# A Mamba decoder layer on one core: the first of sixteen products of each scan step on ScalarE

## The chip, the cores and the metric

The kernel runs on one NeuronCore of a Trainium2 chip. The metric is the device time of one execution in microseconds (us); the kernel before takes 3092.49 us (median of three runs). TensorE (PE) multiplies matrices, VectorE (DVE), ScalarE (ACT) and GpSimd (POOL) do elementwise work, and SyncE (SP) issues the transfers. Each engine runs its own program in order; they meet at semaphores.

## What is computed

The reference is a decoder layer with three parts: a selective state space layer (Mamba), a cross attention, and a small gated LoRA, each followed by a layer norm over a residual sum. The input has 16 sequences of 128 tokens with 1024 features. The change touches the state space part alone. There, with D_IN = 2048 channels and N = 16 states a channel:

```python
dt = jax.nn.softplus(ts @ W_dt.T + b_dt)
A = -jnp.exp(A_log.astype(jnp.float32))

def step(state, inp):
    dt_t, B_t, C_t, u_t = inp
    dA = jnp.exp(dt_t[..., None] * A)
    state = state * dA + (dt_t * u_t)[..., None] * B_t[:, None, :]
    y = jnp.einsum('bdn,bn->bd', state, C_t)
    return (state, y)
```

So the output of a channel at a token is a sum over 16 state indices: y = sum over n of C[n] times state[n]. The product at n = 0 starts this sum, the fifteen others add to it.

## The kernel before

The 16 sequences go in 4 groups of 4 (`GB = 4`), the 2048 channels in 16 tiles of 128. A scan step `s` of the program (there are `NS = 16`) is one group with four channel tiles (`QD = 4`), and within it an unrolled loop runs over the state index `n` from 0 to 15. For each index:

- POOL (`pool_step`, L1085) writes dt·u·B for the four tiles into one of four buffers `hb`.
- ACT (`act_step`, L937) writes four exponentials exp(dt·A), one a channel tile, into PSUM banks 0 and 1 by turns. Exponential `i` waits for the scan two before it, which frees its bank.
- DVE (`dve_scan`, L1159) runs four recurrences along the tokens, one a channel tile; each waits for its exponential.
- PE (`turn(b)` in `pe_step`, L511) transposes the scanned states, four blocks of 128x128 for each sequence `b`, so that tokens lie on the partitions; sequences 0 and 2 go to bank 2, sequences 1 and 3 to bank 3. A turn waits until the bank's last reader has read it.
- DVE (`dve_acc`) multiplies the turned states of sequences 0, 1 and 2 (`OWN = 3`) by C[n], a scalar a partition, and adds them into `acc`: at n = 0 a plain product (L1171, TENSOR_SCALAR), from n = 1 on product and sum (L1174, SCALAR_TENSOR_TENSOR).
- Sequence 3 goes another way: ACT (`act_part`, L781) makes the product, into `acc` at n = 0 and into one of two buffers `part` otherwise, and POOL (`pool_sums`, L1042) adds it.

The engines work at different indices at a time. In round `n` DVE does the products of index n and the scans of index n + 2, written as products of sequences 0 and 1, scans of tiles 0 and 1, product of sequence 2, scans of tiles 2 and 3 (`dve_step`), then what `dve_between` puts there. ACT in round `n` makes the exponentials of index n (those of DVE's round n - 2), each followed by what the table in `act_between` gives it, and ends the round with the product of sequence 3 of index n - 2.

PE fills the time between the turns with other matmuls from a fixed table (`ORDER`, `SIZES`, `pe_filler`): the input projections X and Z (L434), the output projection O (L458) and dt (L446). At n = 1 and n = 11 it also does the small projection `pe_ssm` (L471), which writes bank 2 and so waits for all three of DVE's products of that index.

At the end of a step PE transposes `acc` back (L544, it waits for DVE's last product and POOL's last sum), and DVE adds u·D (L1266) and multiplies by the gate (L1276, semaphore `fin`). The first filler of the next step (L434) needs a bank that the first `fin` frees. Every fourth step DVE copies the C values of the next group into `cg` (L1248) just before index 0. In steps 5, 9 and 13 the layer norm statistics (L1193) stand on DVE between index 0 and index 1.

After the scan steps comes a second phase, the attention and the LoRA for each of 16 sequences, which the change leaves alone. Below, "boundary s" is the stretch in which step s begins (s from 0 to 15); product (n,b), turn (n,b), scan (n,i) and exponential (n,i) name index n with sequence b or channel tile i.

## Time and profile before

| | us |
|---|---|
| median of 3 runs | 3092.49 |
| lowest and highest run | 3089.86 and 3093.56 |
| the profiled execution | 3095.74 |
| its span, first to last instruction | 3093.7 |
| busy: PE, DVE, ACT, POOL | 2757.5, 2602.0, 1657.8, 1848.4 |
| mean granted TensorE clock | 0.950 of full speed |

The busy times are sums over the span; two engines can both be busy nearly all the time, and which of them sets the pace changes from stretch to stretch. A timeline row gives the start and the length of a group of like instructions in a row on one engine; a value in square brackets is the time that the engine stood idle before it, and who ended that. Lengths of neighbouring instructions overlap a little, so what an instruction costs in a row of them is read from the distance of the starts. A matmul in 32 bit takes two records, so `x10` at L434 are five matmuls of 512 columns; a transpose takes one.

### The profile page before, as it was taken

How to read it: one execution, taken by the hardware profiler on the slowest of the kernel's cores; microseconds unless marked ns; L12 is line 12 of the kernel's file. 1: busy time of each engine (PE TensorE's matmuls, PEld its weight loads, DVE VectorE, ACT ScalarE, POOL GpSimd, SP SyncE). 2: the span in 40 equal slices, each digit the busy share in tenths (PEclk: the TensorE clock that was granted, in tenths of full speed). 3: DMA queues.
4: the chain of work that ended last, by engine and by line, in shares of the span. 5: the costliest groups of instructions: out<-in, count | busy, mean ns of one | idle time of the engine just before them, and what ended most of it. 6: DMA issues, size and time to landing. Idle time of an engine off the chain costs nothing.

```text
span 3093.7 us, 34749 instructions
## 1 busy us (share of the span) xinstructions
PE 2757.5 (89%) x10928; PEld 1560.5 (50%) x10928; DVE 2602.0 (84%) x3602; ACT 1657.8 (54%) x2766; POOL 1848.4 (60%) x820
## 2 busy tenths in 40 slices
PE   8968899999989999998999887888878999999996
PEld 4535555555545555554555454554434555555553
DVE  2359998999999999999999999999945777787775
ACT  2346555565655656555565654655514555555553
POOL 1158787777878787786877887888821221222221
PEclk9988899999999999999999998889979999999998
DMA  5442323424252342424333322322121211111110
GB/s 173 130 104 79 107 82 91 144 83 134 79 157 84 103 136 82 132 84 153 89 98 100 96 84 90 119 84 72 48 69 35 89 54 61 61 54 54 61 61 21
DMA packets 132873, 281.28 MB, mean 91 GB/s; under 512 B 12528, under 2 KB 12656, under 8 KB 132224
## 3 DMA queue, kind: packets, MB, share of 16 engines
q1 hardware_dynamic: 132736, 279.59, 30.1%
q8 instruction: 70, 1.15, 0.2%
q14 instruction: 67, 0.55, 0.1%
HBM read 245.86 MB, written 33.69 MB: 90 GB/s over the span
## 4 chain that ended last, share of the span: by engine, by line
PE 49%; DVE 37%; issue 10%; ACT 2%; DMA 1%; POOL 0%; DVEq 0%; SPq 0%; ACTq 0%; POOLq 0%
DVE arena L1159 20%; PE banks L434 14%; DVE arena L1174 8%; PE banks L458 7%; PE banks L511 6%; PE banks L599 4%; PE banks L642 4%; PE banks L555 3%; PE banks L580 3%; PE banks L471 2%; PE banks L610 2%; DVE arena L1115 2%; PE banks L570 2%; DVE banks L1266 1%; DVE rbuf L1187 1%
## 5 line engine op out<-in xcount | busy, mean ns | idle before, releaser
L1159 DVE TENSOR_TENSOR_SCAN arena<-banks,arena 128x512 f32<-128x512 f32 x1024 | 1191.5, 1205 | 11.4 <-POOL arena L1085 11.1
L1085 POOL TENSOR_TENSOR arena<-arena 128x2048 f32<-128x2048 f32 x256 | 1161.7, 4538 | 58.4 <-PE banks L511 58.3
L937 ACT ACTIVATE banks<-arena,a_sb 128x508 f32<-128x508 f32 x1024 | 700.3, 684 | 822.5 <-DVE arena L1159 822.5
L434 PE MATMUL banks<-arena 128*128 128x512 f32 x2048 | 957.2, 605 | 20.2 <-DMA arena<-in_xT 8.2
L511 PEld LDWEIGHTS banks<-ident,arena 128*128 128x128 f32 x4096 | 501.1, 147 | 404.3 <-issue 226.0
L511 PE MATMUL banks<-ident,arena 128*128 128x128 f32 x4096 | 580.8, 286 | 126.6 <-DVE arena L1174 103.2
L1174 DVE SCALAR_TENSOR_TENSOR arena<-banks,cg,arena 128x512 f32<-128x512 f32 x720 | 511.0, 737 | 92.8 <-PE banks L511 91.4
L434 PEld LDWEIGHTS banks<-arena 128*128 128x128 f32 x2048 | 372.7, 195 | 371.9 <-issue 354.8
L458 PE MATMUL banks<-arena 128*128 128x512 f32 x1024 | 497.0, 621 | 46.5 <-DVE arena L1115 22.4
L1042 POOL TENSOR_TENSOR arena<-arena 128x512 f32<-128x512 f32 x240 | 305.1, 1271 | 360.2 <-ACT arena L781 356.6
L1096 POOL TENSOR_TENSOR arena<-arena 128x512 f32<-128x512 f32 x128 | 141.2, 1103 | 465.7 <-DVE arena L1322 465.7
L458 PEld LDWEIGHTS banks<-arena 128*128 128x128 f32 x1024 | 191.0, 200 | 241.6 <-issue 179.1
L1115 DVE SCALAR_TENSOR_TENSOR arena<-banks,taps,arena 128x508 f32<-128x508 f32 (+2 forms) x192 | 141.7, 738 | 125.3 <-ACT arena L698 120.8
L781 ACT ACTIVATE arena<-banks,cg 128x512 f32<-128x512 f32 x256 | 171.1, 668 | 15.7 <-PE banks L511 15.7
L1307 DVE TENSOR_REDUCE arena<-banks 128x8 f32<-128x512 f32 x128 | 88.2, 689 | 107.4 <-PE banks L599 107.4
L1046 POOL TENSOR_TENSOR arena<-arena 128x512 f32<-128x512 f32 x64 | 81.4, 1272 | 150.9 <-ACT arena L712 150.9
L965 ACT ACTIVATE arena<-arena 128x512 f32<-128x512 f32 x128 | 80.7, 630 | 152.5 <-DVE arena L1311 151.9
L599 PE MATMUL banks<-arena 128*128 128x512 f32 x256 | 133.9, 605 | 1.1 <-DVE rbuf L1187 1.1
L555 PE MATMUL banks<-arena 128*128 128x512 f32 x256 | 122.3, 601 | 0.0
L1105 POOL TENSOR_TENSOR ve<-ve,mhalf 128x1 f32<-128x1 f32 x32 | 17.3, 540 | 174.1 <-DVE ve L1348 174.1
L580 PE MATMUL banks<-arena 128*128 128x512 f32 x256 | 121.2, 596 | 0.0
L642 PE MATMUL banks<-arena 128*128 128x512 f32 x256 | 117.2, 602 | 0.7 <-issue 0.7
(131 smaller groups left out, 2769.6 us busy)
## 6 DMA issues: line engine op xcount, KB each, us to landing
arena<-b_scratch SPq DMA_DIRECT2D x128, 512.0 KB, 5.2
arena<-in_WinX SPq DMA_DIRECT2D x128, 256.0 KB, 2.8
arena<-in_WinZ SPq DMA_DIRECT2D x128, 256.0 KB, 2.8
arena<-in_WoutT SPq DMA_DIRECT2D x32, 1024.0 KB, 5.8
u_scratch<-arena SPq DMA_DIRECT2D x64, 256.0 KB, 5.3
arena<-u_scratch SPq DMA_DIRECT2D x16, 1024.0 KB, 9.6
arena<-x_scratch SPq DMA_DIRECT2D x32, 512.0 KB, 3.4
arena<-in_xT SPq DMA_DIRECT2D x14, 1024.0 KB, 8.0
```

Source lines behind the costliest of these rows:

```text
L434: last = nc.tensor.matmul(home(kind, i), wr[w % 2][:, k, :], x[:, k, :], start=(k == 0), stop=(k == KC - 1))
L458: last = nc.tensor.matmul(home("O", i), yq[:, k, b * P:(b + 1) * P], w[:, k, :], start=(k == 0), stop=(k == QD - 1))
L511: last = nc.tensor.transpose(bank(2 + b % 2)[:, i * P:(i + 1) * P], hb[n % 4][:, i * GT + b * P:i * GT + (b + 1) * P], ident[:, :])
L555: last = nc.tensor.matmul(bank(2 + h), wk[:, o * P:(o + 1) * P], cn[:, h * HALF:(h + 1) * HALF], start=True, stop=True)
L580: last = nc.tensor.matmul(bank(6), cT[:, t, :], ekT[:, t, :], start=(t == 0), stop=(t == NT - 1))
L599: nc.tensor.matmul(bank(t % 2), x1[:, t * P:(t + 1) * P], wq, start=True, stop=True)\
L642: last = nc.tensor.matmul(bank(5 + 2 * h), mt[:, o, :], qs[:, o, h * HALF:(h + 1) * HALF], start=(o == 0), stop=(o == OT - 1))
L937: nc.scalar.activation(by_seq(bank(i % 2))[:, :, 1:SEQ], by_seq(dt[s % 2][:, i, :])[:, :, 1:SEQ], ACT.Exp, scale=a_sb[:, QD * q + i, n:n + ...
L1042: nc.gpsimd.tensor_tensor(v, v, part[:, n % 2, :], ALU.add).then_inc(S["sum_ok"], 1)
L1085: nc.gpsimd.tensor_tensor(hb[n % 4].rearrange("p (i t) -> p i t", i=QD), dtu, brep[n // 2 % 4][:, n % 2:n % 2 + 1, :].broadcast_to([P, QD, ...
L1159: nc.vector.tensor_tensor_scan(h, bank(i % 2), h, 0.0, ALU.mult, ALU.add)\
L1174: last = nc.vector.scalar_tensor_tensor(acc[:, b, :], bank(2 + b % 2), c, acc[:, b, :], ALU.mult, ALU.add)
```

## The change

All four products of index 0 go to ACT. They leave DVE's program (three a step), and ACT's own at the end of the round n = 2 is replaced by the fourth of a new function `act_first`. The first two stand in front of the third exponential of index 2, the third in front of the fourth exponential, the fourth behind it. They write `acc` and count in a new semaphore `first_ok`. DVE's program begins its sums at index 1. Counts of `acc_ok` and `part_ok` are renumbered to fifteen a step. No transfer is added or removed, and the rows of PE and POOL stay in their order; what changes there is whom they wait for: turns (0,2), (0,3), (1,0) and (1,1) wait for ACT's copies where they waited for DVE's products.

```diff
 def turn(b):
-    if b == 1:
-        after(pe, "part_ok", U)
+    if n == 0 and b >= 2:
+        pe.wait_ge(S["first_ok"], GB * s + b - 1)
+    elif n == 1 and b < 2:
+        pe.wait_ge(S["first_ok"], GB * s + b + 3)
+    elif b == 1:
+        after(pe, "part_ok", (N - 1) * s + max(n - 1, 0))
     else:
-        after(pe, "acc_ok", OWN * U + (0, 0, 1, 2)[b])
+        after(pe, "acc_ok", OWN * (N - 1) * s + OWN * max(n - 1, 0) + (0, 0, 1, 2)[b])
...
+        def act_first(act, s, b):
+
+            act.wait_ge(S["t_done"], QD * N * s + b + 1)
+            if b == 0:
+                after(act, "yt_mm", QD * s)
+                act.wait_ge(S["cg_ok"], s // NQ + 1)
+            nc.scalar.activation(acc[:, b, :], bank(2 + b % 2), ACT.Identity, scale=cg[:, b, 0:1])\
+                .then_inc(S["first_ok"], 1)
+
         def act_part(act, s, n):
 
             act.wait_ge(S["t_done"], QD * (N * s + n + 1))
-            if n == 0:
-                after(act, "yt_mm", QD * s)
-                act.wait_ge(S["cg_ok"], s // NQ + 1)
-                dst = acc[:, OWN, :]
-            else:
-                after(act, "sum_ok", (N - 1) * s + max(n - 2, 0))
-                dst = part[:, n % 2, :]
-            nc.scalar.activation(dst, bank(3), ACT.Identity, scale=cg[:, OWN, n:n + 1])\
+            after(act, "sum_ok", (N - 1) * s + max(n - 2, 0))
+            nc.scalar.activation(part[:, n % 2, :], bank(3), ACT.Identity, scale=cg[:, OWN, n:n + 1])\
                 .then_inc(S["part_ok"], 1)
...
                     act_between(act, s, n, i)
-                if U >= 2:
+                    if n == 2 and i == 1:
+                        act_first(act, s, 0)
+                        act_first(act, s, 1)
+                    if n == 2 and i == 2:
+                        act_first(act, s, 2)
+                if n == 2:
+                    act_first(act, s, OWN)
+                elif U >= 2:
                     act_part(act, (U - 2) // N, (U - 2) % N)
...
         def dve_acc(dve, s, n, b):
 
-            k = OWN * (N * s + n) + b
+            k = OWN * ((N - 1) * s + n - 1) + b
             dve.wait_ge(S["t_done"], QD * (N * s + n) + b + 1)
-            c = cg[:, b, n:n + 1]
-            if n == 0:
-                if b == 0:
-                    after(dve, "yt_mm", QD * s)
-                    dve.wait_ge(S["cg_ok"], s // NQ + 1)
-                last = nc.vector.tensor_scalar(acc[:, b, :], bank(2 + b % 2), c, None, ALU.mult)
+            if n == 1:
+                dve.wait_ge(S["first_ok"], GB * s + b + 1)
             else:
                 dve.wait_ge(S["acc_ok"], k - OWN + 1)
...
                     for b in range(2 * part, min(2 * part + 2, OWN)):
-                        dve_acc(dve, s, n, b)
+                        if n > 0:
+                            dve_acc(dve, s, n, b)
```

How it moves instructions is seen best at boundary 1. On DVE, the kernel before, from the last gate products (L1276) over index 0 (products L1171) to index 1 (products L1174); L1159 are the scans:

```order
L1276 TENSOR_TENSOR arena<-banks,arena 128x512 x2
L1171 TENSOR_SCALAR arena<-banks,cg 128x512 x2
L1159 SCALAR_TENSOR_TENSOR arena<-banks,arena 128x512 x2
L1171 TENSOR_SCALAR arena<-banks,cg 128x512
L1159 SCALAR_TENSOR_TENSOR arena<-banks,arena 128x512 x2
L1174 SCALAR_TENSOR_TENSOR arena<-banks,cg,arena 128x512 x2
L1159 SCALAR_TENSOR_TENSOR arena<-banks,arena 128x512 x2
```

The same place in the changed kernel, whose lines are shifted (the gate product is L1287, the scan L1174, product and sum L1185):

```order
L1287 TENSOR_TENSOR arena<-banks,arena 128x512 x2
L1174 SCALAR_TENSOR_TENSOR arena<-banks,arena 128x512 x4
L1185 SCALAR_TENSOR_TENSOR arena<-banks,cg,arena 128x512 x2
L1174 SCALAR_TENSOR_TENSOR arena<-banks,arena 128x512 x2
L1185 SCALAR_TENSOR_TENSOR arena<-banks,cg,arena 128x512
L1174 SCALAR_TENSOR_TENSOR arena<-banks,arena 128x512 x2
```

The three products are gone, and the four scans of index 2 stand together. On ACT, the kernel before at the same boundary, from the exponential and the sigmoid piece (L712) of round 1 to round 2 with its four exponentials (L937) and the product of sequence 3 (L781):

```order
L712 ACTIVATE arena<-arena 128x512
L937 ACTIVATE banks<-arena,a_sb 128x4x127
L781 ACTIVATE arena<-banks,cg 128x512
L937 ACTIVATE banks<-arena,a_sb 128x4x127 x4
L781 ACTIVATE arena<-banks,cg 128x512
L937 ACTIVATE banks<-arena,a_sb 128x4x127 x4
```

And in the changed kernel, where the exponential is L944, the new copy L781 and the product of sequence 3 of the other indices L788:

```order
L716 ACTIVATE arena<-arena 128x512
L944 ACTIVATE banks<-arena,a_sb 128x4x127
L788 ACTIVATE arena<-banks,cg 128x512
L944 ACTIVATE banks<-arena,a_sb 128x4x127 x2
L781 ACTIVATE arena<-banks,cg 128x512 x2
L944 ACTIVATE banks<-arena,a_sb 128x4x127
L781 ACTIVATE arena<-banks,cg 128x512
L944 ACTIVATE banks<-arena,a_sb 128x4x127
L781 ACTIVATE arena<-banks,cg 128x512
L944 ACTIVATE banks<-arena,a_sb 128x4x127 x4
```

Three copies are new; exponential (2,2) stands behind two of them and (2,3) behind the third.

## Rows read from the trace of the kernel before

**Rows 1.** The page: busy time by engine, and the chain that ended last.

```profile
PE 2757.5 (89%) x10928; PEld 1560.5 (50%) x10928; DVE 2602.0 (84%) x3602; ACT 1657.8 (54%) x2766; POOL 1848.4 (60%) x820
PE 49%; DVE 37%; issue 10%; ACT 2%; DMA 1%; POOL 0%; DVEq 0%; SPq 0%; ACTq 0%; POOLq 0%
```

**Rows 2.** Windows: stretch, length, busy PE, PEld, DVE, ACT, POOL, granted clock, DMA.

```profile
458.00:590.00 132.00, 123.13 (x496) 70.81 (x496) 123.33 (x144) 75.62 (x123) 103.31 (x39) 0.97 0.39 112
474.00:481.00 7.00, 6.84 (x21) 4.88 (x22) 2.90 (x4) 3.73 (x7) 5.75 (x2) 0.52 0.13 45
```

**Rows 3.** Waits in the scan steps (190 to 2290 us): total, times, longest.

```profile
ACT banks L937 <- DVE arena L1159: 822.5, 685, 10.0
DVE arena L1174 <- PE banks L511: 91.4, 77, 3.6
DVE arena L1159 <- POOL arena L1085: 11.1, 5, 9.2
```

**Rows 4.** Groups by line: count, busy time, mean of one in ns, idle time before.

```profile
L1171 DVE TENSOR_SCALAR arena<-banks,cg 128x512 f32<-128x512 f32 x48 | 34.1, 737 | 0.5
```

**Rows 5.** Timeline of DVE at boundary 2: start, length, count, idle time before.

```profile
463.38 1.40 DVE L1171 TENSOR_SCALAR arena<-banks,cg 128x512 f32<-128x512 f32 x2
464.70 2.33 DVE L1159 TENSOR_TENSOR_SCAN arena<-banks,arena 128x512 f32<-128x512 f32 x2
466.94 0.73 DVE L1171 TENSOR_SCALAR arena<-banks,cg 128x512 f32<-128x512 f32 x1
467.58 2.33 DVE L1159 TENSOR_TENSOR_SCAN arena<-banks,arena 128x512 f32<-128x512 f32 x2
469.83 1.39 DVE L1174 SCALAR_TENSOR_TENSOR arena<-banks,cg,arena 128x512 f32<-128x512 f32 x2
...
481.58 1.41 DVE L1174 SCALAR_TENSOR_TENSOR arena<-banks,cg,arena 128x512 f32<-128x512 f32 x2 [3.10 <-PE banks L511]
```

**Rows 6.** Timeline of PE at boundary 2; the last row is L471 at boundary 3.

```profile
458.99 1.04 PE L511 MATMUL banks<-ident,arena 128*128 128x128 f32 x8
460.41 4.56 PE L434 MATMUL banks<-arena 128*128 128x512 f32 x10 [0.38 <-DVE arena L1276]
464.80 1.04 PE L511 MATMUL banks<-ident,arena 128*128 128x128 f32 x8
465.68 2.74 PE L434 MATMUL banks<-arena 128*128 128x512 f32 x6
468.25 0.60 PE L511 MATMUL banks<-ident,arena 128*128 128x128 f32 x4
...
474.16 3.73 PE L471 MATMUL banks<-arena 128*128 128x96 f32 x16 [2.23 <-DVE arena L1174]
...
608.12 2.02 PE L471 MATMUL banks<-arena 128*128 128x96 f32 x16 [2.23 <-DVE arena L1174]
```

**Rows 7.** Timeline of ACT at boundary 2.

```profile
456.69 0.69 ACT L937 ACTIVATE banks<-arena,a_sb 128x508 f32<-128x508 f32 x1 [0.43 <-DVE arena L1159]
465.94 0.69 ACT L937 ACTIVATE banks<-arena,a_sb 128x508 f32<-128x508 f32 x1 [8.56 <-DVE arena L1159]
...
467.69 0.67 ACT L781 ACTIVATE arena<-banks,cg 128x512 f32<-128x512 f32 x1
```

**Rows 8.** Timelines of boundaries 1, 5, 12: turn (1,0) and product (1,0).

```profile
335.55 0.60 PE L511 MATMUL banks<-ident,arena 128*128 128x128 f32 x4
336.19 1.41 DVE L1174 SCALAR_TENSOR_TENSOR arena<-banks,cg,arena 128x512 f32<-128x512 f32 x2
...
868.52 0.60 PE L511 MATMUL banks<-ident,arena 128*128 128x128 f32 x4
875.49 0.75 DVE L1174 SCALAR_TENSOR_TENSOR arena<-banks,cg,arena 128x512 f32<-128x512 f32 x1
...
1803.03 0.60 PE L511 MATMUL banks<-ident,arena 128*128 128x128 f32 x4
1804.94 1.39 DVE L1174 SCALAR_TENSOR_TENSOR arena<-banks,cg,arena 128x512 f32<-128x512 f32 x2
```

More of the change, by code:

```diff
@@ L97 @@
 wdt_loaded wo_loaded u_loaded0 u_loaded1 r_loaded brep_loaded0 brep_loaded1 brep_loaded2 brep_loaded3
-dt_mm dt_abs dt_exp dt_ln dt_ok dtu_ok cg_ok exp_ok bm_ok scan_ok t_done acc_ok part_ok sum_ok yt_mm fin1 fin
+dt_mm dt_abs dt_exp dt_ln dt_ok dtu_ok cg_ok exp_ok bm_ok scan_ok t_done first_ok acc_ok part_ok sum_ok yt_mm fin1 fin
 z_mm z_copied z_exp z_ln z_sig z_ok o_mm r_added ln_stats ln_aggr ln_eps ln_rstd ln_shift ln_ok x1_stored
@@ L528, in pe_step @@
                 if n == 1 and (has_x(s - 1) or s == 0):
-                    pe.wait_ge(S["acc_ok"], OWN * (U + 1))
+                    pe.wait_ge(S["acc_ok"], OWN * ((N - 1) * s + n))
                     pe_ssm(pe, (LEAD + QD * s) // 2 - 1)
                 if n == 4 and q == NQ - 1 and s + 1 < NS:
-                    pe.wait_ge(S["acc_ok"], OWN * (U + 1))
+                    pe.wait_ge(S["acc_ok"], OWN * ((N - 1) * s + n))
                     pe_rows(pe, g + 1)
                 if n == 11 and has_x(s):
-                    pe.wait_ge(S["acc_ok"], OWN * (U + 1))
+                    pe.wait_ge(S["acc_ok"], OWN * ((N - 1) * s + n))
                     pe_ssm(pe, (LEAD + QD * s) // 2)
                 pe_filler(pe, s, 2 * n + 1)
-            pe.wait_ge(S["acc_ok"], OWN * N * (s + 1))
+            pe.wait_ge(S["acc_ok"], OWN * (N - 1) * (s + 1))
             pe.wait_ge(S["sum_ok"], (N - 1) * (s + 1))
@@ L1038, in pool_sums @@
                 return
-            pool.wait_ge(S["part_ok"], N * s + n + 1)
+            pool.wait_ge(S["part_ok"], (N - 1) * s + n)
+            pool.wait_ge(S["first_ok"], GB * (s + 1))
             after(pool, "sum_ok", (N - 1) * s + n - 1)
@@ L1162, in dve_acc @@
         def dve_acc(dve, s, n, b):
-            k = OWN * (N * s + n) + b
+            k = OWN * ((N - 1) * s + n - 1) + b
             dve.wait_ge(S["t_done"], QD * (N * s + n) + b + 1)
-            c = cg[:, b, n:n + 1]
-            if n == 0:
-                if b == 0:
-                    after(dve, "yt_mm", QD * s)
-                    dve.wait_ge(S["cg_ok"], s // NQ + 1)
-                last = nc.vector.tensor_scalar(acc[:, b, :], bank(2 + b % 2), c, None, ALU.mult)
+            if n == 1:
+                dve.wait_ge(S["first_ok"], GB * s + b + 1)
             else:
                 dve.wait_ge(S["acc_ok"], k - OWN + 1)
-                last = nc.vector.scalar_tensor_tensor(acc[:, b, :], bank(2 + b % 2), c, acc[:, b, :],
-                                                      ALU.mult, ALU.add)
-            last.then_inc(S["acc_ok"], 1)
+            nc.vector.scalar_tensor_tensor(acc[:, b, :], bank(2 + b % 2), cg[:, b, n:n + 1], acc[:, b, :],
+                                           ALU.mult, ALU.add).then_inc(S["acc_ok"], 1)
         def dve_out(dve, s, c):
@@ L1245, in dve_step @@
             if s % NQ == 0:
-                after(dve, "acc_ok", OWN * N * s)
-                after(dve, "part_ok", N * s)
+                after(dve, "acc_ok", OWN * (N - 1) * s)
+                after(dve, "part_ok", (N - 1) * s)
                 nc.vector.tensor_copy(cg[:, :, :], ssn[:, :, R + N:SS]).then_inc(S["cg_ok"], 1)
```

## The prediction

> **What bounds the kernel now.** I read the page first. PE is busy for 89% of the span and DVE for 84%, and the chain that ended last is 49% PE, 37% DVE and 2% ACT [rows 1]. So DVE's time counts, but not everywhere, and ACT's hardly anywhere. The second phase has none of the instructions that change. The windows of a whole scan step tell more: in the 132 us of step 2 DVE is busy 123.33, PE 123.13 and ACT 75.62 [rows 2]. PE and DVE are level. What DVE no longer does can be won only where PE does not hold it back at that moment, and the average does not say where that is. Next come the waits: ACT's exponentials stood idle 822.5 us for a scan to free their bank, while DVE's products waited 91.4 us in all for PE's turns, in 77 places, and its scans 11.1 us for POOL [rows 3]. DVE goes its own pace nearly always and is stopped by PE in some places. So the answer lies in the timelines of the 16 boundaries.
>
> **What goes.** 48 products of 737 ns leave DVE, 34.1 us with next to no idle time before them [rows 4]. What they cost in the row is less, since neighbours overlap. By the starts at boundary 2 the first two take 464.70 - 463.38 = 1.32 and the third 467.58 - 466.94 = 0.64, together 1.96 us a boundary [rows 5], 31.4 us over 16. That is the most the removal can be worth by itself.
>
> **What of it DVE can use.** I write boundary 2 anew. DVE is done with the gate products at 463.38 and has only the four scans in front of it. Two scans take 466.94 - 464.70 = 2.24, so one takes 1.12: they start at 463.38, 464.50, 465.62 and 466.74, and DVE is free at 467.86. Before, it came to the product (1,0) at 469.83 [rows 5]. That product needs turn (1,0) of PE, which starts at 468.25 and lasts 0.60, so it ends at 468.85 [rows 6]. Does that turn come sooner too? PE's stretch before it has no gap: the first filler starts at 460.41, released by the first gate product, then turns at 464.80, filler at 465.68, turn at 468.25 [rows 6]. Its start depends on DVE work that lies ahead of the removed products, and the work in it is unchanged. So turn (1,0) stays where it is. At boundary 1 the product follows a turn that it waits for: 335.55 + 0.60 = 336.15, product at 336.19, thus 0.04 later [rows 8]. With this, product (1,0) of boundary 2 starts at 468.89 and not at 469.83: 0.94 us are won and DVE stands idle 1.03. The second product finds its turn done, since the two turns start 0.44 apart (four of the eight in 1.04 less 0.60) [rows 6].
>
> **The other boundaries** differ in how late DVE was against turn (1,0). I went through all 16:
> - Boundary 1 has no slack at all (336.19 against 336.15) [rows 8]: gain 0.
> - Boundaries 0, 2, 3, 6, 7, 10, 11, 14 and 15, nine of them, are like boundary 2: 0.94 each, 8.5 us.
> - Boundaries 4, 8 and 12 come later by the copy of C. At 12 the turn ends at 1803.03 + 0.60 and the product started at 1804.94, so 1804.94 - 1803.67 = 1.27 [rows 8], three times, 3.8 us.
> - Boundaries 5, 9 and 13 have the layer norm statistics between index 0 and 1. At 5 the turn started at 868.52 and the product at 875.49 [rows 8]. PE is far ahead, the whole 1.96 is won, three times, 5.9 us.
>
> The sum is **18.2 us**.
>
> **What carries it to the end.** Behind product (1,0) come its neighbours, then product (1,2), and PE stands idle for that: 2.23 us before the small projection at boundary 2 [rows 6]. This pause shrinks to about 1.3 and is not used up, so PE, and through it POOL and the transfers, move forward with DVE. POOL stops scans for 11.1 us in all, and 9.2 of them are one place at the start [rows 3]; its later rows wait for ACT's product and so move too. The transfers are issued from PE's and POOL's progress; no queue is passed by anything. PE's L511 rows change only in what they wait for: turns (0,2) and (0,3) need two copies that are long done, turn (1,0) the third and turn (1,1) the fourth.
>
> **What is added.** On ACT, 48 copies of 0.67 us [rows 7], 32.2 us on an engine that is idle 56 of 132 us a step [rows 2]; the fourth copy only moves. At boundary 2 ACT's last exponential starts at 456.69 and the next at 465.94, with 8.56 us idle between [rows 7]. The first two copies fit in there: their turns start at 458.99 [rows 6] and end by about 460.0, so they are done at about 460.9. Exponential (2,2) now follows scan (2,0) by 1.24 as before (465.94 against 464.70) and runs from 464.62 to 465.31, before scan (2,2) at 465.62. The third copy waits for turn (0,2), 464.80 + 0.60 = 465.40, and runs until about 466.1. Exponential (2,3) comes behind it, some 466.06 to 466.75, where scan (2,3) wants it at 466.74. That is even; a delay of a tenth would only eat DVE's new idle time. The fourth copy ends near 467.4, before turn (1,1) at about 468.7. So I cost ACT's part at nothing: what covers it is the 1.03 us for which DVE waits anyway. Boundaries 4, 8 and 12 (and 0) are closer, since the copies can start only when C is copied, just before DVE starts its scans: two copies take 1.3 of the 1.56 us (2.24 less the 0.69 of an exponential) that are there. At boundaries 5, 9 and 13, without that idle time, the tenth counts: between 0 and 0.2 us each.
>
> **The clock.** In the window from 474 to 481 us PE's granted clock is 0.52, the lower level of 1.2 GHz, after a pause of 2.23 us; the small projection there took 3.73 us, at boundary 3 after the same pause 2.02 [rows 2, 6]. DVE paid: it waited 3.10 us at 481.58 [rows 5]. So such a fall costs 1.7 us. Of the twelve like places (the steps 0 to 11) I found this full price at boundaries 2 and 4. Shorter pauses make it no likelier; between both falls vanishing (3.4 us more gained) and two new ones (3.4 less) I take none, as equal pauses gave both outcomes. The Trainium skill (TensorE: Matmul & The Clock Gate, HAM oscillation) says that idle gaps before bursts of matmuls are what lets the gate close, so that bursts start cold. By that rule alone the sum would be 3.4 us larger; the trace agrees only in part, since the pause of 2.23 us closed the gate at one boundary and not at the next.
>
> **Sum.** The profiled execution took 3095.74 us, so I expect 3095.74 - 18.2 = 3077.5 in its terms. The median of the runs lies 3.25 below the profiled one, so the forecast for the median is **3074.3 us**, 0.6% less. A measurement of this kernel tells a change from none at about 0.2%, 6.2 us, so "faster" begins at 3086.3.
>
> **The rivals.**
> - *PE sets the pace everywhere.* PE is busy 89% and DVE 84% [rows 1], and DVE waits 91.4 us for PE [rows 3]. If PE's stretch carried through each step without a pause, DVE would only wait more and nothing would be won: 3092.5. Against it stand PE's pause for DVE behind boundary 2 and 3 [rows 6] and the slack at boundaries 2, 5 and 12. The Trainium skill (Perfetto Trace Analysis, Identifying the Most-Contended Engine) would have the engine with the highest occupancy relieved first, which speaks against a change on DVE; but it also says that PE is not to be judged by matmul occupancy, and PE's weight loads are at 50% [rows 1]. Chance 0.08.
> - *The full 31.4 us.* Turn (1,0) would have to come earlier too, or DVE to make up its wait later in the step. Time 3061.1. Nothing speaks for it but that I may have read PE's stretch wrongly. Chance 0.05.
> - *The clock falls more often.* If PE's lower clock came at ten more boundaries, 1.7 us each, 17 us would be lost and the time were 3091. Chance 0.03.
> - *ACT's queue becomes the bound* (slower). The place is exponential (2,2), which now stands behind two copies that wait for PE's turns (0,0) and (0,1), with turns (0,2) and (1,0) waiting for ACT in return. It begins to cost when the second copy ends later than 463.38 + 1.56 = 464.94; I reckon 460.9, so 4.0 us are spare at twelve boundaries and 0.2 at four. It makes the kernel slower from 4.0 + 1.96 = 6.0 us of lateness on. One us beyond that at each boundary would give 3092.5 + 16 = 3108. Chance 0.04.
> - *The change doesn't do what it says.* The rows of DVE and ACT show the three products gone and three copies new, so this has no chance of its own.
>
> **How the numbers follow.** The forecast has 0.80, with a range of its own from 3067 to 3083: 7.3 below, 3.4 us of clock and some 4 of the 13.2 us (31.4 less 18.2) that I reckon as wait; 8.7 above, a quarter of the gain (4.5) lost in places that I take to be rigid, and the 3.7 us over which the runs spread. The full gain has 0.05, the even cases 0.08 and 0.03, the slower one 0.04. So faster is 0.85, within 0.2% 0.11, slower 0.04. The forecast's own range leaves 2 in 10 out, and it is the range.
>
> **What would show it.** In the changed profile DVE should have 48 instructions less in the scan steps and some 34 us less busy time, ACT 48 more and 32 us more. Product (1,0) should wait for PE's turn about 1 us at nine boundaries, 0.7 at three, 2 at boundary 1 and not at all at 5, 9 and 13; DVE's waits for L511 should grow from 91.4 by about 13. Step to step, boundaries 5, 9 and 13 should be 2 us nearer to what follows, boundary 1 nothing. The pause before L471 should be 1.3 and not 2.23. The forecast is wrong if scan (2,2) or (2,3) waits for an exponential by more than 0.3 us, if turns (0,2) to (1,1) wait for ACT, if PE's granted clock over the steps differs, or if the waits further back in a step grow by what the boundary won.

## The result, and the profile after

| | before | after |
|---|---|---|
| median of the runs (lowest to highest), us | 3093.74 (3089.86 to 3098.13) | 3085.42 (3078.67 to 3091.12) |
| profiled execution, us | 3095.74 | 3078.67 |
| its span, us | 3093.7 | 3076.8 |
| mean granted TensorE clock in it | 0.950 | 0.950 |

The ratio is 0.997, with a 95% interval from 0.996 to 0.998. The change makes the kernel faster by 8.3 us; I had forecast 18.2, and the median of 3085.42 lies 2.4 us outside my range of 3067 to 3083. The profiled execution is 17.1 us faster than that of before, but it is also the fastest of the ten of the changed kernel, and the time given for them is 6.8 us above it. So there are two results to explain: the 17.1 us, which is near the forecast, and the rest, which is not there in the median.

The page of the changed kernel, busy times and the shares of the chain that ended last (before in [rows 1]):

```profile
PE 2756.6 (90%) x10928; PEld 1560.0 (51%) x10928; DVE 2572.2 (84%) x3554; ACT 1685.2 (55%) x2814; POOL 1848.9 (60%) x820
...
PE 52%; DVE 34%; issue 10%; ACT 2%; DMA 1%; POOL 0%; DVEq 0%; SPq 0%; ACTq 0%; POOLq 0%
```

DVE's busy time falls by 29.8 us (I had some 34) and ACT's grows by 27.4 (I had 32); the counts change by 48 each, as forecast. The chain moves from DVE to PE by 3% of the span, though PE does the same work. The waits over the scan steps, engine, line and who was waited for, with us in total, times and the longest (before in [rows 3]):

```profile
ACT banks L944 <- DVE arena L1174: 727.7, 636, 10.0
DVE arena L1185 <- PE banks L515: 110.3, 93, 3.6
```

DVE's products wait 110.3 us for PE's turns in 93 places, where they waited 91.4 in 77. ACT still waits hundreds of us for scans. The timeline of DVE at boundary 2 (before in [rows 5]; start, length, and in brackets the idle time before):

```profile
459.19 4.59 DVE L1174 TENSOR_TENSOR_SCAN arena<-banks,arena 128x512 f32<-128x512 f32 x4
464.70 1.41 DVE L1185 SCALAR_TENSOR_TENSOR arena<-banks,cg,arena 128x512 f32<-128x512 f32 x2 [0.93 <-PE banks L515]
...
473.30 1.41 DVE L1185 SCALAR_TENSOR_TENSOR arena<-banks,cg,arena 128x512 f32<-128x512 f32 x2 [1.61 <-PE banks L515]
```

From the end of the gate products to product (1,0) it is now 464.70 - 459.19 = 5.51 us, and it was 469.83 - 463.38 = 6.45 [rows 5]. That is 0.94 less, and DVE stands idle 0.93 in front of the product. PE at the same boundary (before in [rows 6]):

```profile
456.22 4.56 PE L434 MATMUL banks<-arena 128*128 128x512 f32 x10 [0.38 <-DVE arena L1287]
460.62 1.04 PE L515 MATMUL banks<-ident,arena 128*128 128x128 f32 x8
461.49 2.74 PE L434 MATMUL banks<-arena 128*128 128x512 f32 x6
464.07 0.60 PE L515 MATMUL banks<-ident,arena 128*128 128x128 f32 x4
...
469.06 2.02 PE L471 MATMUL banks<-arena 128*128 128x96 f32 x16 [1.36 <-DVE arena L1185]
```

Turn (1,0) starts at 464.07 and ends at 464.67; the product starts at 464.70. From the filler at 456.22 to this turn there is no gap. The pause ahead of the small projection L471 is 1.36 us, and was 2.23. ACT (before in [rows 7]):

```profile
452.51 0.69 ACT L944 ACTIVATE banks<-arena,a_sb 128x508 f32<-128x508 f32 x1 [0.42 <-DVE arena L1174]
455.44 1.27 ACT L781 ACTIVATE arena<-banks,cg 128x512 f32<-128x512 f32 x2 [2.24 <-PE banks L515]
460.44 0.69 ACT L944 ACTIVATE banks<-arena,a_sb 128x508 f32<-128x508 f32 x1 [3.74 <-DVE arena L1174]
461.25 0.69 ACT L781 ACTIVATE arena<-banks,cg 128x512 f32<-128x512 f32 x1
461.84 0.68 ACT L944 ACTIVATE banks<-arena,a_sb 128x508 f32<-128x508 f32 x1
462.45 0.68 ACT L781 ACTIVATE arena<-banks,cg 128x512 f32<-128x512 f32 x1
```

The first two copies (L781) end at 456.71 and ACT waits another 3.74 us for the scan. No scan or turn of this boundary waits for ACT. DVE at boundaries 1, 5 and 12 (before in [rows 8]):

```profile
329.63 1.22 DVE L1174 TENSOR_TENSOR_SCAN arena<-banks,arena 128x512 f32<-128x512 f32 x1 [1.32 <-ACT banks L944]
331.78 1.41 DVE L1185 SCALAR_TENSOR_TENSOR arena<-banks,cg,arena 128x512 f32<-128x512 f32 x2 [0.93 <-PE banks L515]
...
868.52 1.41 DVE L1185 SCALAR_TENSOR_TENSOR arena<-banks,cg,arena 128x512 f32<-128x512 f32 x2
...
1792.16 1.41 DVE L1185 SCALAR_TENSOR_TENSOR arena<-banks,cg,arena 128x512 f32<-128x512 f32 x2 [0.85 <-PE banks L515]
```

**Where the 17.1 us lie.** I cut each step of both traces at the starts of two scans: the boundary from scan (1,0) to scan (6,0), and the rest from there to the next step's scan (1,0). The last rest, of step 15, ends where its last scan starts. In us, steps 0 to 15:

```
boundary, before: 39.4 43.5 47.0 45.1 45.8 51.6 43.8 45.1 44.2 51.9 43.8 44.4 40.6 45.5 41.0 41.0
boundary, after:  36.7 43.8 42.9 44.2 42.9 51.1 42.9 44.2 42.9 50.6 42.9 42.9 40.3 43.7 38.9 40.6
rest, before:     81.8 89.8 87.0 88.4 87.0 88.5 88.5 88.4 88.5 88.5 88.5 77.9 80.8 80.6 79.0 64.5
rest, after:      80.2 90.0 90.1 89.4 89.9 88.6 88.5 88.4 86.9 88.5 90.0 78.8 80.5 80.4 80.8 64.8
```

The boundaries are 22.1 us shorter, the rests 8.1 us longer. The start gives 0.5 and the second phase, which has no part in the change, 2.3. Together 22.1 - 8.1 + 0.5 + 2.3 = 16.8, of the 16.9 us by which the two spans differ. That the whole comes near the forecast of 18.2 is in part luck: the boundaries gave 3.9 more than forecast, the start and the second phase 2.8 that had no term, and the rests took 8.1 back.

A rest holds none of the changed instructions. What differs in it is the granted clock. Step 3 as a whole, from turn (0,0) to turn (0,0), and its rest; columns: stretch, length, then busy us and count of PE, PE's loads, DVE, ACT and POOL, granted clock, DMA share, GB/s. Before:

```profile
593.00:726.40 133.40, 123.65 (x509) 70.37 (x508) 126.66 (x153) 79.85 (x139) 105.25 (x41) 0.99 0.37 112
638.00:726.40 88.40, 83.50 (x348) 47.68 (x346) 83.90 (x97) 56.78 (x93) 75.25 (x31) 1.00 0.41 122
```

After:

```profile
587.80:721.40 133.60, 125.09 (x510) 71.82 (x509) 125.02 (x150) 81.59 (x142) 105.35 (x41) 0.97 0.35 112
631.90:721.30 89.40, 84.87 (x346) 48.71 (x345) 83.93 (x97) 56.79 (x93) 75.26 (x31) 0.98 0.37 120
```

DVE has three instructions less and 1.64 us less to do, and the step is 0.2 us longer. PE is busy 1.44 us longer with the same work, at a mean clock of 0.97 where it was 0.99. In all scan steps PE is at the lower of its two levels (1.2 GHz) for 221.7 us before and 221.3 after, added up from the trace's record of the clock between the same scans (below, a fall of the clock is a stretch at this level). But it lies elsewhere:

| at the lower level, us | before | after |
|---|---|---|
| boundaries of steps 0 to 10 | 43.5 | 30.6 |
| rests of steps 0 to 10 | 52.5 | 68.8 |
| boundaries of steps 11 to 15 | 47.8 | 37.5 |
| rests of steps 11 to 15 | 77.9 | 84.4 |

Some 23 us moved from the boundaries to the rests. Of the 8.1 us by which the rests grew, 5.6 lie in steps 0 to 10 and 2.5 in steps 11 to 15, and both parts have this counterpart.

### The profile page after: what moved, and what is told of

Same layout as the page of the kernel before. It is cut to its first block, busy times and chain, and to the rows that moved or that the text cites. A ratio compares the mean times of both kernels' runs of the same rounds, so it can differ in the third digit from the quotient of the medians.

```text
span 3076.8 us, 34749 instructions
## 1 busy us (share of the span) xinstructions
PE 2756.6 (90%) x10928; PEld 1560.0 (51%) x10928; DVE 2572.2 (84%) x3554; ACT 1685.2 (55%) x2814; POOL 1848.9 (60%) x820
## 4 chain that ended last, share of the span: by engine, by line
PE 52%; DVE 34%; issue 10%; ACT 2%; DMA 1%; POOL 0%; DVEq 0%; SPq 0%; ACTq 0%; POOLq 0%
DVE arena L1174 19%; PE banks L434 17%; DVE arena L1185 8%; PE banks L458 6%; PE banks L515 6%; PE banks L603 4%; PE banks L646 4%; PE banks L559 3%; PE banks L584 3%; PE banks L614 2%; PE banks L471 2%; DVE arena L1130 2%; PE banks L574 2%; DVE rbuf L1197 1%; PE banks L653 1%
## 5 line engine op out<-in xcount | busy, mean ns | idle before, releaser
L1174 DVE TENSOR_TENSOR_SCAN arena<-banks,arena 128x512 f32<-128x512 f32 x1024 | 1190.5, 1205 | 12.9 <-POOL arena L1100 11.2
L944 ACT ACTIVATE banks<-arena,a_sb 128x508 f32<-128x508 f32 x1024 | 700.1, 684 | 729.0 <-DVE arena L1174 727.7
L1185 DVE SCALAR_TENSOR_TENSOR arena<-banks,cg,arena 128x512 f32<-128x512 f32 x720 | 511.3, 737 | 111.6 <-PE banks L515 110.3
L458 PE MATMUL banks<-arena 128*128 128x512 f32 x1024 | 495.4, 620 | 46.8 <-DVE arena L1130 22.4
L458 PEld LDWEIGHTS banks<-arena 128*128 128x128 f32 x1024 | 190.0, 199 | 238.6 <-issue 175.9
L1130 DVE SCALAR_TENSOR_TENSOR arena<-banks,taps,arena 128x508 f32<-128x508 f32 (+2 forms) x192 | 141.8, 738 | 124.8 <-ACT arena L702 120.3
L788 ACT ACTIVATE arena<-banks,cg 128x512 f32<-128x512 f32 x240 | 160.5, 669 | 15.4 <-PE banks L515 15.4
```

What stands on the lines that cost most here:

```text
L458: last = nc.tensor.matmul(home("O", i), yq[:, k, b * P:(b + 1) * P], w[:, k, :], start=(k == 0), stop=(k == QD - 1))
L944: nc.scalar.activation(by_seq(bank(i % 2))[:, :, 1:SEQ], by_seq(dt[s % 2][:, i, :])[:, :, 1:SEQ], ACT.Exp, scale=a_sb[:, QD * q + i, n:n + ...
L1174: nc.vector.tensor_tensor_scan(h, bank(i % 2), h, 0.0, ALU.mult, ALU.add)\
L1185: nc.vector.scalar_tensor_tensor(acc[:, b, :], bank(2 + b % 2), cg[:, b, n:n + 1], acc[:, b, :], ALU.mult, ALU.add).then_inc(S["acc_ok"], 1)
```

## The experiments

**Is it the same again?** Both kernels once more, unedited.

> The kernel before once more, for a second profiled execution. Theory A: its time scatters by 8 us as it did, the boundaries are the same to 3 us in both of its profiles, and the difference between its two profiles lies in stretches with a lower clock. Theory B: its boundaries differ by more than 5 us between the two profiles.

> The changed kernel once more, unaltered, for a second profiled execution and more times. Theory A (the boundaries win 18 us in every execution, and falls of PE's clock elsewhere in the steps, which vary from execution to execution, take back about 10 of it on average): the times scatter over 3078 to 3091 us around 3085, a higher time goes with a lower mean clock, and in the new profile the boundaries are again some 20 us shorter than before while the stretches behind them are longer by 5 to 15 us. Theory B (the boundaries themselves win less in most executions, and the first profile was an exception): the new profile shows boundaries that are only about 10 us shorter in all, with products (1,0) waiting over 1.5 us for their turn.

> The changed kernel a third time, unaltered, hoping for another chip, since ten executions at first gave a median of 3085.4 us and five later ones 3078.6. Theory A (the gain at the boundaries is fixed, what scatters is the number of falls of PE's clock in the steps, each of 3.4 us at the lower level costing about 1.55 us): whatever the median is, the boundaries of steps 2 to 15 keep their lengths to 0.3 us where no fall lies in them, and the time goes with the mean clock, 0.001 of it being worth about 3 us. Theory B (some other part of the chip's state sets the time): a higher median with the same mean clock of 0.950 or 0.951.

> The changed kernel a fourth time, for the spread over executions beside the kernel before: 3078 to 3090 us, 3 us more for each 0.001 less of mean clock; at a mean clock of 0.950 some 3080 to 3082, 12 us under the kernel before at the same clock.

| run | median (lowest to highest), us | ratio to before [95%] |
|---|---|---|
| before_again | 3093.99 (3090.55 to 3101.87) | 1.0001 [0.9992, 1.0010] |
| after_again | 3078.62 (3078.33 to 3081.61) | 0.9956 [0.9943, 0.9970] |
| after_third | 3082.05 (3077.92 to 3090.23) | 0.9974 [0.9961, 0.9986] |
| after_fourth | 3079.34 (3077.78 to 3081.20) | 0.9954 [0.9940, 0.9968] |

The boundaries of steps 2 to 15 agree to 0.1 us in all four profiles of the changed kernel; boundary 0 of after_fourth is 1.0 us longer and its boundary 1 0.3 shorter. Those of the two profiles of before agree to 0.2. The time does not repeat as well: the interval of after_fourth reaches from 0.9940 to 0.9968, that of the first result from 0.996 to 0.998. Over all 27 executions of the changed kernel the median is 3081.3; over 78 of before, 3093.5. That is 12.2 us, and I take it as the best value for the change. The four comparisons, each with executions of before made beside it, gave 8.3, 15.0, 10.3 and 14.2. Within the 27 the time goes with the mean clock that each execution was granted:

| mean clock | executions | us |
|---|---|---|
| 0.947 | 4 | 3087.4 to 3090.2 |
| 0.948 | 4 | 3084.2 to 3084.8 |
| 0.949 | 2 | 3086.1 to 3086.5 |
| 0.950 | 8 | 3077.8 to 3082.0 |
| 0.951 | 8 | 3077.9 to 3081.6 |

The one left over had 0.931 and took 3091.1. A straight line through the table gives 2.3 us for each 0.001; through the 68 executions of before whose clock is on record it gives 1.2. No slow execution was profiled, so what lies behind a mean clock of 0.947 inside the steps is not shown. The runs were made on several chips. On the one of after_again and after_fourth all ten executions have 0.950 or more; on that of after_third three of seven have less, and of the first ten eight have less. So the chip may have a part in it, which was not tried apart.

**Do the copies cost anything?** no_copies leaves the terms of n = 0 of sequences 0, 1 and 2 out; ACT makes only the fourth copy, and DVE's plain product is that of index 1.

```diff
-                    if n == 2 and i == 1:
-                        act_first(act, s, 0)
-                        act_first(act, s, 1)
-                    if n == 2 and i == 2:
-                        act_first(act, s, 2)
...
-                dve.wait_ge(S["first_ok"], GB * s + b + 1)
+                nc.vector.tensor_scalar(acc[:, b, :], bank(2 + b % 2), cg[:, b, n:n + 1], None, ALU.mult)\
+                    .then_inc(S["acc_ok"], 1)
```

The waits of turns (0,2), (0,3) and (1,0) for a reader of their bank go too, since nobody reads it.

> The changed kernel without the products of index 0 of sequences 0, 1 and 2: ACT makes only the fourth copy, and DVE's first instruction of the sum is a plain product of index 1. It leaves out the terms n = 0 of the sum for three of four sequences. Theory (the copies cost nothing, they lie in ACT's idle time): the same as the changed kernel within 3 us, 3083 to 3087. Rival (ACT's copies in front of exponentials (2,2) and (2,3) cost part of the gain): faster than the changed kernel by 5 us or more, 3080 or less.

Measured 3080.20 (3078.07 to 3083.57), ratio 0.9960 [0.9947, 0.9974]. The changed kernel beside it had 0.9956. The 32 us of ACT's work, and PE's waits for it, cost nothing that can be measured.

**Does their place matter?** late_copies puts all four behind the last exponential of the round.

```diff
-                    if n == 2 and i == 1:
-                        act_first(act, s, 0)
-                        act_first(act, s, 1)
-                    if n == 2 and i == 2:
-                        act_first(act, s, 2)
                 if n == 2:
-                    act_first(act, s, OWN)
+                    for b in range(GB):
+                        act_first(act, s, b)
```

> The changed kernel with all four copies of ACT behind the fourth exponential of index 2, none ahead of the third. Theory (the place counts, since turns (0,2) to (1,1) of PE wait for the copies): exponential (2,3) starts as scan (2,1) ends, the first copy about 0.6 us later, some 465.4 on the scale of the kernel before, so turn (0,2) starts 1.2 us later than 464.8, turn (0,3) waits another 1.2 us, and turn (1,0) comes some 2.5 us later than in the changed kernel: 2.5 us lost at 13 boundaries, 32 us, 3110 us, slower than the kernel before. Rival (PE has slack there, the place of the copies is free): within 3 us of the changed kernel.

Measured 3107.74 (3104.63 to 3110.50), ratio 1.0050 [1.0037, 1.0063]: slower than before. ACT, then PE, then DVE of this kernel at boundary 6, three timelines:

```profile
1007.78 1.25 ACT L781 ACTIVATE arena<-banks,cg 128x512 f32<-128x512 f32 x2
1009.20 1.27 ACT L781 ACTIVATE arena<-banks,cg 128x512 f32<-128x512 f32 x2 [0.17 <-PE banks L515]
```

```profile
1008.51 1.24 PE L515 MATMUL banks<-ident,arena 128*128 128x128 f32 x8 [2.12 <-ACT arena L781]
```

```profile
1012.79 1.41 DVE L1181 SCALAR_TENSOR_TENSOR arena<-banks,cg,arena 128x512 f32<-128x512 f32 x2 [3.44 <-PE banks L515]
```

Turn (0,2) can't be written before the first copy has read bank 2, and waits 2.12 us; product (1,0) waits 3.44 us for its turn, where it waited 0.93. The same wait is 3.44 to 5.13 us at thirteen boundaries and none at 5, 9 and 13. The rival of ACT's queue is real, with its place and its sign, and what keeps it away in the changed kernel is the place of the first two copies in ACT's idle 3.74 us.

**Is it PE's stretch that caps the gain?** By my working the wait of 0.93 us in front of product (1,0) comes from three fillers of PE that stand before turn (1,0). sizes_after moves one of them behind the turn; sizes_before does the same in the kernel before, where DVE should not care.

```diff
-SIZES = [5, 3, 2, 2] + [3, 3] + [3, 4] + ...
+SIZES = [5, 2, 3, 2] + [3, 3] + [3, 4] + ...
```

> The changed kernel with one filler product of PE moved from ahead of turn (1,0) to behind turn (1,1) (table 5,3,2,2 becomes 5,2,3,2). Turn (1,0) then comes 0.86 us earlier. Theory: PE's stretch is what holds DVE at the boundary, so this wins another 9 x 0.86 + 3 x 0.69 + 0.86 = 10.7 us over the changed kernel in a profile, median near 3075. Rival (PE's pause before the small projection is no real reserve, the moved product is paid for there): 0 to 3 us, median 3082 to 3085.

> The changed kernel with the moved filler once more, for its ratio on another chip: 3058 to 3065 us, ratio 0.990. Its boundaries are 0.9 us shorter than the changed kernel's at 13 places (11 us), the other 7 to 10 us come from steps that lose fewer products to the lower clock; if the second part is chance of the moment it could be 0 to 10 here, 3061 to 3071.

> The kernel before with the same filler product moved (5,3,2,2 becomes 5,2,3,2), as a control. There DVE itself sets the pace up to product (1,0) and has 1 us of slack against turn (1,0), so an earlier turn wins nothing but at boundary 1. Theory (PE's stretch binds only once the products are gone): 0 to 3 us faster than the kernel before, 3090 to 3093, plus what the clock does, up to 5 us either way. Rival (the moved product wins by itself, in either kernel): 15 us or more, 3078 or less.

| run | median (lowest to highest), us | ratio to before [95%] |
|---|---|---|
| sizes_after | 3060.95 (3058.29 to 3064.47) | 0.9899 [0.9884, 0.9914] |
| sizes_again | 3063.57 (3058.51 to 3065.21) | 0.9900 [0.9885, 0.9916] |
| sizes_before | 3090.17 (3084.17 to 3093.09) | 0.9985 [0.9976, 0.9994] |

DVE of sizes_after at boundary 2:

```profile
456.49 4.58 DVE L1174 TENSOR_TENSOR_SCAN arena<-banks,arena 128x512 f32<-128x512 f32 x4
461.14 1.41 DVE L1185 SCALAR_TENSOR_TENSOR arena<-banks,cg,arena 128x512 f32<-128x512 f32 x2
```

and its waits over the scan steps:

```profile
DVE arena L1185 <- PE banks L515: 90.1, 73, 3.3
```

From the gate products to product (1,0) it is 4.65 us instead of 5.51, and DVE's waits are back to 90.1 us. DVE of sizes_before at the same place:

```profile
464.10 1.40 DVE L1171 TENSOR_SCALAR arena<-banks,cg 128x512 f32<-128x512 f32 x2
465.42 2.32 DVE L1159 TENSOR_TENSOR_SCAN arena<-banks,arena 128x512 f32<-128x512 f32 x2
...
470.55 1.38 DVE L1174 SCALAR_TENSOR_TENSOR arena<-banks,cg,arena 128x512 f32<-128x512 f32 x2
```

and PE of sizes_before:

```profile
468.53 1.25 PE L511 MATMUL banks<-ident,arena 128*128 128x128 f32 x8 [0.25 <-DVE arena L1171]
```

There the product comes 470.55 - 464.10 = 6.45 us after the gate products, to the hundredth what it was, though its turn (468.53 + 0.60) is done 1.42 us before. So PE's stretch caps the changed kernel at this place and not the one before. The table of fillers alone is worth 3 us, the products alone 12, both together 30 to 33. I had expected 10.7 us from the moved filler, and it gave 18 to 20. The expected part is there in both profiles: all boundaries together are 11.4 us shorter in sizes_after than in the changed kernel, and 12.5 in sizes_again. The surplus varies with the clock: the rests of steps 0 to 10 add up to 963.1 us in sizes_after, with 49.2 us at the lower level, to 968.8 with 62.9 in sizes_again, and to 970.7 with 68.8 in the changed kernel.

**Is it the clock that lengthens the rests?** If it is only a matter of where the falls come, another start should change it without any change of the work. shift_after and shift_before let GpSimd clear `acc` once before the first scan step.

```diff
+            if s == 0:
+                nc.gpsimd.memset(acc[:, :, :], 0.0)
```

> The changed kernel with one GpSimd memset of 128x2048 ahead of the first product of scan step 0, which starts all the scan steps about 2 us later. If only a delay, the time is that of the changed kernel plus the delay, 3080 to 3081. Theory A: the pauses of PE now fall at other moments against the chip's clock control, so the number of falls in the steps changes and the time departs from that sum by multiples of about 1.5 us, by 3 to 9 us in all, either way. Theory B: within 1 us of the sum.

> The same delay of about 2 us in the kernel before. If only a delay: about 3096. Theory A: it departs from that too, by 3 to 9 us either way, so that the difference of the two kernels is not 15 us at every start of the steps but anything from 8 to 25. Theory B: 3096 within 1 us, and a difference of 15 us to the delayed changed kernel.

shift_after: 3074.98 (3069.99 to 3086.61), ratio 0.9948 [0.9932, 0.9963]; its scans begin 1.7 to 2.8 us later than in the four traces of the changed kernel. shift_before: 3093.53 (3090.60 to 3095.93), ratio 1.0003 [0.9994, 1.0012]; 0.5 to 0.9 us later than in the two traces of before, less than I had expected. More work at the start, and the changed kernel is 6 to 7 us faster than without it, while the kernel before does not move. The intervals of shift_after and of after_third, which was measured beside it, overlap, so the medians alone don't show it. The trace says more. Steps 3 and 4 of shift_after, and the rest of step 3:

```profile
591.90:722.80 130.90, 122.03 (x510) 69.99 (x509) 124.83 (x150) 81.57 (x142) 105.36 (x41) 1.00 0.37 115
722.80:852.70 129.90, 121.28 (x507) 69.65 (x506) 123.45 (x145) 78.09 (x127) 105.30 (x41) 1.00 0.35 98
636.10:722.80 86.70, 81.81 (x338) 46.54 (x337) 83.28 (x97) 56.78 (x93) 75.25 (x31) 1.00 0.40 124
```

With the same instructions (DVE x150, PE x510) as in the changed kernel, step 3 takes 130.9 us at a clock of 1.00, where it took 133.6 at 0.97. Its rest is 86.7 and not 89.4. Counted from scan (1,0) of step 3, every instruction of PE, DVE, ACT and POOL starts in the two traces at the same time to 0.02 us, up to 46.6 us. Then the changed kernel is at the lower level for 3.4 us, and behind that it is some 1.4 us later, on all four engines, until 97.8 us, where the next 3.4 us at the lower level make it 2.7. Nothing else parts the two traces in this step. The first of these falls comes with PE's pause before L479, first the changed kernel, then shift_after:

```profile
627.48 1.09 PE L479 MATMUL banks<-ident,arena 128*96 128x128 f32 x4 [2.23 <-DVE arena L1185]
```

```profile
631.59 0.64 PE L479 MATMUL banks<-ident,arena 128*96 128x128 f32 x4 [2.23 <-DVE arena L1187]
```

The pause is 2.23 us in both; the clock was at the lower level from 626.91 to 630.32 in the one and did not fall in the other. Over seven traces the rests of steps 0 to 10 follow the time that PE spends in them at the lower level:

```
at the lower level, us:   49.0   49.2   52.5   55.9   62.9   68.8   69.4
rests of steps 0-10, us: 963.5  963.1  965.1  965.8  968.8  970.7  971.9
kernel: sizes_before, sizes_after, before, shift_after, sizes_again, after, after_fourth
```

That is (971.9 - 963.1) / (69.4 - 49.2) = 0.44 us for each us at the lower level, and kernels with and without the three products lie on one line. Single rests say the same. In thirteen of the fourteen traces, all but that of sizes_two below, a rest of steps 1 to 10 takes 86.7 to 87.0 us with nothing at the lower level, 88.0 to 88.7 with 3.4 us, and 89.4 to 90.1 with 6.8 us, in either kernel. So the lengthening belongs to the clock and not to DVE's work.

**A version that beats both.** In the middle of a step PE and DVE also wait for each other, in the changed kernel and in sizes_after alike. At the filler L458 of n = 7 PE waits for DVE's L1130 to free its bank, and the next turn, queued behind that filler, keeps DVE waiting in return. sizes_two takes one more filler out of the last slot of n = 1 and puts it back at n = 12, so that every filler between comes one product later and the turn goes first.

```diff
-SIZES = [5, 3, 2, 2] + [3, 3] + [3, 4] + [3, 3] * 2 + [3, 4] + [3, 3] + [3, 4] * 2 + [3, 3] + [2, 2] + [3, 3] * 2 + [3, 4] * 2
+SIZES = [5, 2, 3, 1] + [3, 3] + [3, 4] + [3, 3] * 2 + [3, 4] + [3, 3] + [3, 4] * 2 + [3, 3] + [2, 2] + [3, 4] + [3, 3] + [3, 4] * 2
```

> The changed kernel with two filler products moved: one from ahead of turn (1,0) to behind turn (1,1), as before, and one from behind the small projection at n = 1 to the end of n = 12, where PE pauses for DVE (table 5,2,3,1 and, at n = 12, 3,4). With one moved, DVE still waits 1.61 us for turn (2,0) at eleven steps. Theory (PE's stretch binds there too): another 0.86 us at eleven steps, 9.5 us under the 3061 to 3064 of one moved product, near 3053. Rival (every later tile of PE comes one product later, and DVE and ACT wait for those): no gain or a loss, 3061 to 3070. The clock adds up to 5 us either way.

Measured 3023.97 (3022.55 to 3028.53), ratio 0.9771 [0.9758, 0.9784]: 37 us less than sizes_after, where I had expected 9.5. The expected part, at the boundaries, is 12.3 us in the profiles. The rest I had not forecast; it lies in the rests of the steps, which are 23.9 us shorter. PE of sizes_after in step 2, where n = 7:

```profile
507.52 2.07 PE L458 MATMUL banks<-arena 128*128 128x512 f32 x2 [2.90 <-DVE arena L1130]
509.39 1.91 PE L515 MATMUL banks<-ident,arena 128*128 128x128 f32 x8
```

DVE of sizes_after there:

```profile
505.20 2.27 DVE L1130 SCALAR_TENSOR_TENSOR arena<-banks,taps,arena 128x508 f32<-128x508 f32 x3
...
510.49 1.60 DVE L1185 SCALAR_TENSOR_TENSOR arena<-banks,cg,arena 128x512 f32<-128x512 f32 x2 [2.42 <-PE banks L515]
```

PE of sizes_two:

```profile
502.31 1.04 PE L515 MATMUL banks<-ident,arena 128*128 128x128 f32 x8
504.52 2.84 PE L458 MATMUL banks<-arena 128*128 128x512 f32 x6 [1.17 <-DVE arena L1130]
```

DVE of sizes_two:

```profile
502.19 2.27 DVE L1130 SCALAR_TENSOR_TENSOR arena<-banks,taps,arena 128x508 f32<-128x508 f32 x3
504.38 0.68 DVE L1165 SCALAR_TENSOR_TENSOR arena<-banks,arena 128x512 f32<-128x512 f32 x1
504.98 1.40 DVE L1185 SCALAR_TENSOR_TENSOR arena<-banks,cg,arena 128x512 f32<-128x512 f32 x2
```

The turn now stands ahead of the filler. DVE does not wait at all (2.42 before), PE waits 1.17 (2.90 before), and the first L458 matmul and its turn, which took 2.07 and 1.91 us at the lower level behind the long pause, are fast. The rests of steps 1 to 10 took 86.7 to 89.8 us in sizes_after; here eight of the ten take 85.8. PE's wait at that filler was 2.48 to 2.90 us in eight steps of sizes_after; it is 1.17 in six of them and under 1 in the other two. The waits for turns come down to:

```profile
DVE arena L1185 <- PE banks L515: 53.7, 69, 3.0
```

The mean clock of the profiled execution is 0.961, and 150.6 us of its scan steps are at the lower level, 204.3 in sizes_after. No run divides the 37 us between waits and clock. By an estimate from the rests of steps 0 to 10, they are 19.3 us shorter with 23.9 us less at the lower level, which at 0.44 makes 10.5 us of clock and 8.8 of waits; but some of the falls came with those waits, so the two go together.

## Where the prediction was right, and where it failed

The median missed the forecast of 3074.3 by 11.1 us. Between the profiled executions the miss is 1.1 (3078.67 for 3095.74 - 18.2); the other 10.0 us come at the step from the profiled execution to the median.

- *The sum over the boundaries* was right in its mechanism. I had 0.94 at nine, 1.27 at three, 1.96 at three and nothing at boundary 1. Up to product (1,0) of boundary 2 it is 0.94 to the hundredth. Whole boundaries gave 0.9 at 3, 6, 7 and 10 and 1.2 at 8, as forecast, and the 16 together 22.1 us for 18.2. Of the difference, boundaries 0, 2 and 4 gave 6.5 more than their terms (2.7 + 4.1 + 2.9 less 3.15), where falls of the clock were gone, and boundaries 5, 9 and 12 gave 3.1 less (0.5 + 1.3 + 0.3 for 5.19); at boundary 5 the lower level lasted 10.2 us and had lasted 6.8. The five others (1, 11, 13, 14, 15) differ by -0.5 to +1.2, in all by +0.7; the clock fell in each of them, and why boundaries 12 and 15 gave less than their terms is not shown. That these errors offset each other is luck.
- *The wait in front of product (1,0)* was forecast at 1 us at nine boundaries, 0.7 at three and none at 5, 9 and 13. It is 0.93, 0.85 and none. At boundary 1 I forecast 2; it is 0.93, since scan (2,3) had waited 1.32 for ACT before. That wait is over my bound of 0.3, but it only takes the place of the other: the turn is the later of the two. All such waits together grew by 18.9 us, and I had 13: the rest is in places further back in a step.
- *ACT's copies cost nothing* was right (no_copies). The slower rival was right in its kind: late_copies is 1.0050 of before.
- *PE sets the pace everywhere* was wrong as a whole and right in places: sizes_after shows that the gain was cut by PE's stretch before turn (1,0), as I had reckoned.
- **What failed first is the step on the clock.** "Shorter pauses make it no likelier; between both falls vanishing (3.4 us more gained) and two new ones (3.4 less) I take none". The term was neither none nor within these bounds: at boundaries 0, 2 and 4 the falls that vanished gave 6.5 us, at three places and not two, and at boundary 2 3.2 us where I had 1.7 for a fall, and the rests, which had no term at all, took 8.1 us back. With the 3.9 us that the boundaries gave over the forecast, the scan steps lost 4.2 us against it. I had looked for falls at the pause behind the boundary alone. They went from there and came in the middle of the steps, where the clock was at the lower level for 52.5 us in the rests of steps 0 to 10 and is now for 68.8. Why just there the runs don't show; that it hangs on when the steps begin, shift_after does. The rule that I had quoted (the Trainium skill, TensorE: Matmul & The Clock Gate, HAM oscillation) gave 3.4 us more gain. For boundaries 0, 2 and 4 the traces agree with its direction, by more; for the steps as wholes they don't, since the time at the lower level inside the scan steps stayed (221.7 and 221.3 us).
- **And, with more weight in the number, the step from the profiled execution to the median.** I took 3.25 us off, the difference of one execution to a median of three of the kernel before. The changed kernel had 6.8 to add. It also spreads more: its profiled execution is the fastest of ten, and their median is 6.8 us above. Between profiled executions the forecast of 18.2 stands beside 17.1; over all executions, beside 12.2; over the first ten of each, beside 8.3. My range of 8.7 us upward allowed for a quarter of the gain lost and the spread of three runs, and the median came 2.4 us above it. Why the ten executions spread towards the slow side is open; what is shown is that eight of them had a mean clock under 0.950.
- "So PE, and through it POOL and the transfers, move forward with DVE" held: no new wait for POOL or for a transfer is among those that grew.

Left open: why the clock falls at one like place and not at the other, and why the first ten executions had lower mean clocks than most of the seventeen after them.

## What to carry to other kernels

When two engines run level and hand work to each other, what is taken off one is worth, at each meeting point, the smaller of what was removed and the slack of the other, and this can be read from starts in the timeline. It held to a tenth of a us at boundaries 3, 6, 7, 8 and 10, the ones in which the clock fell in neither kernel; in the others the difference was 0.2 to 3.2 us, either way. Then the other engine's order should be tuned anew at the same points: here the table of PE's fillers alone gave 3 us, the removed products alone 12, both together 30 to 33, and with one more shift of the fillers 3095.78 - 3023.97 = 71.8. In sizes_two it paid to let a turn go ahead of a filler that waits for a buffer, where the engine that frees the buffer waits for that turn next. Work given to an engine with idle time is free only in the right slot of its queue: the same copies, one or two exponentials later, cost 3107.7 - 3081.3 = 26.4 us.

## What I had not expected of the hardware

- The granted clock of PE is part of the balance. At equal work a step took 130.9 us at 1.00 and 133.6 at 0.97, and in the rests of steps 0 to 10 each us at the lower level costs some 0.44 us.
- A start 1.7 to 2.8 us later, by an instruction that only adds work, took step 3 of the changed kernel from 0.97 to 1.00. The same pause of 2.23 us of PE went with 3.4 us at the lower level in the one trace and with none in the other.
- The kernel's time spreads with the mean granted clock: from 3077.8 to 3091.1 us in 27 executions of the same program. Two medians of the same kernel, of ten and of five executions, lay 6.8 us apart (3085.42 and 3078.62), so a result of some 0.3% needs tens of executions here.
